# Two combine stages dissolved into the attentions that follow them, a third staging slot, and scores of two head pairs issued together

## The chip, the cores and the metric

One core of one Trainium2 chip runs the whole program in one launch. The time is device microseconds (us) from start to end of an execution; the value compared is the median of several executions of the same kernel. PE is the matmul engine (TensorE), DVE the vector engine, ACT the scalar engine with its function tables, POOL the GpSimd engine, SP the engine that issues most DMAs. SBUF is the on-chip memory, PSUM the eight banks into which PE writes.

## The reference, cut to what matters

Everything is fp32. x is [16 batches, 112 rows, 256], the context is [16, 375, 256]. Eight blocks follow each other, each of the form x = x + block(layernorm(x)):

- L0_xattn, a "focused" linear attention over the context; L0_ffn, a gated mixture of 8 experts, top 2 of them per row, added to the row with softmax weights;
- L1_xattn, an attention whose scores pass a tanh before the softmax ("tanh attention"); L1_ffn, a shared feed-forward with low-rank expert terms;
- L2_xattn, softmax attention with 16 heads of 64 ("wide"); L2_ffn, again 8 experts and top 2, but its sum passes a layernorm of its own;
- L3_xattn, softmax attention with 16 heads of 16 and a mask ("narrow"); L3_ffn, a ternary feed-forward.

The two mixtures, and the norm that follows each:

```python
# L0_ffn: xn = layernorm(x); f = layernorm(xn)*gamma+beta; top 2 experts, weights p
x = x + p0*y[expert0] + p1*y[expert1]   # rows beyond an expert's capacity get 0
# L2_ffn: h = layernorm(x)
x = x + layernorm(h + p0*y[expert0] + p1*y[expert1], eps=1e-12) * ln_w + ln_b
# the next block (L1_xattn or L3_xattn) begins with layernorm(x) of that x
# L3_xattn, per batch and head
scores = q @ k.T / 4
scores = where(mask == 0, -1e9, scores)
out = softmax(scores) @ v
```

## The kernel before, in words

`program` (L2852) runs twelve stages, with a barrier of all engines between two of them (`core.clear`, L115): focused attention, route, run_experts and combine of L0_ffn, tanh attention, shared experts, wide attention, route, run_experts and combine of L2_ffn, narrow attention, ternary feed-forward. Inside a stage each engine has its own program, written out by hand for batch 0 to 15, and semaphores order them. Nothing of the next stage starts before the barrier.

**Routing.** `route` (L2279) normalises x and computes for every row its two experts, its slots in a DRAM buffer and the weights p. `picked` is ready when the experts are chosen; PE then makes the running counts (`cum`, L2540), DVE the slots (`slots_done`), and POOL writes the rows out with 32 indirect DMAs ("puts", L2364). **Experts.** `run_experts` (L2548) reads blocks of rows, runs both matmuls and stores y in DRAM (`ybuf`). **Combine.** `combine` (L2744) fetches each row's two results with 32 indirect DMAs on POOL ("gathers", L2787, two per batch, a ring of four batches), adds them with two scalar_tensor_tensor on DVE (L2812, L2814), and takes the statistics (bn_stats, bn_aggr). For L2_ffn (`norm`) the sum goes to `xf`, one Sqrt on ACT follows when all 16 batches are summed (L2799), and then six DVE instructions a batch (L2827 to L2833) normalise, scale, add ln_b, add x, and take statistics again.

**Keys and values made early.** Later attentions need projections of the context. PE makes them as "parts" in earlier stages, where it has room, ACT copies each part out of PSUM (`take`). `KeysValues` (L2064) keeps those of the narrow attention in SBUF: 4 parts a batch, batches 0 to 9 in route of L2_ffn ("r_"), 10 to 15 in its combine ("c_"). `SpilledKeysValues` (L2142) makes 8 of the 16 batches of the wide attention, 14 parts a batch (8 of K, 6 of V), and stores them in DRAM from two staging slots: batches 0 to 3 in the focused attention, 4 to 6 in route of L0_ffn, 7 in its combine. ACT waits for a slot's earlier store before it writes the slot, and each stage waits for its stores before it ends (`wait_stored`, L2205). In `route` the parts stand in three places of PE's program: one beside each batch (BESIDE), eight before the `cum` matmul (AHEAD), the rest behind it (BEHIND). In route of L2_ffn, DVE also prepares the ternary weights (`tw.prepare`, L1721, two reductions at L1727), and PE sums them (`tw.sum`, L1719) before the last four parts.

**Tanh attention** (L568). ACT takes all deviations in one Sqrt (L661), then per batch six tanh (L679) and six exponentials (L671). PE's program for a batch is scores 0 and 1, transposes of the next batch's x (L751), the projection of batch b-2 (L788), scores, products (L775), the spreading of sums (L783), scores, products. DVE's: normalise the next x (L697), copy its transpose (L703), residual of b-2 (L720 and `keep`, L99), copy the products' sum (L709), reciprocal (L714), divide (L716). POOL builds the masked queries `qbd` (L648) and copies values (L655).

**Narrow attention** (`softmax_attention` with wide False, L830). Per pair of heads PE issues the scores of the pair (L1375, two matmuls of 375 columns on two of four banks), turns the probabilities of earlier heads (L1387, transposes), runs slot jobs (q, x, z, y) and every four heads the products (L1410). `scores` waits until DVE has read the banks of the pair before (`low_done`). DVE takes each head's masked minimum (L1230) and writes the masked scores to `ssb`, a ring of four; ACT takes the exponential (L1165) into `p_sb`, a ring of eight. DVE also copies most turned probabilities (L1241), and once a batch does the residual, divide and normalise. PE's program is:

```python
def body(b, h):
    for pair in range(0, H, 2):
        scores(b, h, pair)
        trail(b, h, pair, LT, turn_p)      # LT = 4 heads behind
        slot_jobs(job, b, h, pair, "kqvxyz")
        trail(b, h, pair + 1, LT, turn_p)
        if (pair - LP) % SIDE == 0:
            trail(b, h, pair, LP, products)  # LP = 8 behind
```

## Time and profile before

| what | value |
|---|---|
| median of three executions | 2900.87 us (2896.5 to 2906.04) |
| profiled execution | 2931.14 us |
| its span in the trace | 2929.4 us |
| mean granted clock of PE | 0.935 of full |
| PE, DVE, ACT, POOL busy | 86%, 47%, 39%, 27% of the span |

Where the stages lie in that span (from the first instructions of each in the trace): focused attention 0 to 310.8 us, route of L0_ffn to 425.8, its experts to 832.5, its combine to 901.8, tanh attention to 1112.5, shared experts to 1274, wide attention to 1905, route of L2_ffn to 2024, its experts to 2296.5, its combine to 2391.8, narrow attention to 2757, ternary feed-forward to the end. The page divides the span in 40 slices of 73 us, and its second part gives the busy tenths of each engine in each slice:

```profile
PE   6999749999956998979999999883999559999786
...
DVE  6988512222232654546643333442111367777665
ACT  4555211111105991234443434331333126666431
POOL 3443140000041210027754444404000401221242
PEclk8999879999977998989999999996999779999898
```

A digit 9 says that the engine was busy for 90% or more of the slice. PE has its weak slices at the routing stages (slices 6 and 28) and at the combines (slices 12, 13, 32 and 33). A busy share says how full an engine is, not what the end of a stage waited for: that is to be read from the chain of instructions in each stage.

### The profile page before, as it was taken

What the parts mean: (1) busy time and instruction counts of PE and PEld (TensorE: products, weight loads), DVE (VectorE), ACT (ScalarE), POOL (GpSimd) and SP (SyncE); (2) the same over time, 40 slices, a digit from 0 to 9 for tenths busy, and PEclk for the clock granted to TensorE, in tenths of its full rate; (3) what the DMA queues carried; (4) which work ended last, traced back from release to release, by engine and by line L of the source; (5) the groups of instructions that cost most, each with busy time, mean ns of one, the idle gap of its engine ahead of it and who ended that gap; (6) DMA issues with size and microseconds to landing.
All of it is one profiled execution on the core that took longest, in us unless ns stands there. A gap on an engine that the chain in (4) does not pass through costs nothing. (4 is left out here: it accounts for less than half of the span.)

```text
span 2929.4 us, 47164 instructions
## 1 busy us (share of the span) xinstructions
PE 2512.4 (86%) x15874; PEld 1754.4 (60%) x15874; DVE 1372.3 (47%) x4867; ACT 1130.7 (39%) x2617; POOL 797.8 (27%) x867
## 2 busy tenths in 40 slices
PE   6999749999956998979999999883999559999786
PEld 4676428888832554647666565562999336666544
DVE  6988512222232654546643333442111367777665
ACT  4555211111105991234443434331333126666431
POOL 3443140000041210027754444404000401221242
PEclk8999879999977998989999999996999779999898
DMA  4222352222023210043310000044888310000000
GB/s 138 82 101 102 133 197 108 93 84 94 24 85 118 67 54 1 1 134 133 113 36 6 11 6 6 1 155 172 322 325 325 127 35 11 8 11 6 1 7 19
DMA packets 69939, 252.57 MB, mean 86 GB/s; under 512 B 16395, under 2 KB 32040, under 8 KB 52264
## 3 DMA queue, kind: packets, MB, share of 16 engines
q1 hardware_dynamic: 60008, 226.24, 22.2%
q0 software_dynamic: 9744, 23.87, 2.6%
q8 instruction: 114, 1.87, 0.3%
q14 instruction: 73, 0.60, 0.1%
HBM read 197.97 MB, written 52.10 MB: 85 GB/s over the span
## 5 line engine op out<-in xcount | busy, mean ns | idle before, releaser
L2732 PE MATMUL L_ffne_up<-L_ffne_xT,L_ffne_wu 128*128 128x128 f32 (+1 forms) x2144 | 389.8, 337 | 7.3 <-DMA L_ffne_wu<-in_L_ffn_up 7.3
L2732 PEld LDWEIGHTS L_ffne_up<-L_ffne_xT,L_ffne_wu 128*128 128x128 f32 x2144 | 328.1, 193 | 54.3 <-DMA L_ffne_wu<-in_L_ffn_up 6.9
L1082 POOL TENSOR_SCALAR L_xattn_p<-L_xattn_p,L_xattn_rec 112x375 f32<-112x375 f32 x256 | 311.8, 1225 | 0.0
L1387 PEld LDWEIGHTS L_xattn_pt<-ident,L_xattn_p 112*125 112x125 f32 x1536 | 197.3, 189 | 166.4 <-ACT L_xattn_p L1165 75.7
L2717 PE MATMUL L_ffne_dn<-L_ffne_wd,L_ffne_hT 128*112 128x256 f32 (+1 forms) x1200 | 266.3, 379 | 1.5 <-issue 1.5
L1387 PE MATMUL L_xattn_pt<-ident,L_xattn_p 112*125 112x112 f32 x1536 | 247.3, 289 | 20.5 <-DVE L_xattn_pt L1241 16.0
L1224 DVE TENSOR_REDUCE L_xattn_least<-L_xattn_s 112x1 f32<-112x375 f32 x256 | 128.4, 543 | 284.7 <-PE L_xattn_s L1375 284.4
L2717 PEld LDWEIGHTS L_ffne_dn<-L_ffne_wd,L_ffne_hT 128*112 128x112 f32 (+1 forms) x1200 | 216.8, 183 | 39.7 <-issue 2.1
L1241 DVE COPY L_xattn_pt<-L_xattn_pt 125x336 f32<-125x336 f32 x448 | 210.6, 497 | 52.6 <-PE L_xattn_pt L1387 52.4
L1165 ACT ACTIVATE L_xattn_p<-L_xattn_s,L_xattn_least 112x375 f32<-112x375 f32 x256 | 145.1, 570 | 186.2 <-DVE L_xattn_least L1224 186.1
L2620 POOL DMA_DIRECT2D L_ffn_ybuf<-L_ffne_y x75 | 40.1, 534 | 641.3 <-DVE L_ffne_y L2670 386.8
L1165 ACT ACTIVATE L_xattn_p<-L_xattn_ssb,L_xattn_least 112x375 f32<-112x375 f32 x256 | 153.8, 602 | 129.9 <-DVE L_xattn_least L1230 129.0
L2642 ACT ACTIVATE L_ffne_sg<-L_ffne_up 128x280 f32<-128x280 f32 x128 | 51.6, 403 | 329.0 <-PE L_ffne_up L2732 329.0
L2644 ACT ACTIVATE L_ffne_hT<-L_ffne_up,L_ffne_b 128x128 f32<-128x128 f32 x280 | 98.9, 366 | 154.9 <-DMA L_ffne_b<-in_L_ffn_b 76.0
L1230 DVE CUSTOM_DVE_ANT_0 L_xattn_ssb<-L_xattn_s,L_xattn_hide 112x375 f32<-112x375 f32 x256 | 130.8, 545 | 57.4 <-issue 37.7
L1080 POOL TENSOR_TENSOR pool_tick<-ident 1x1 f32<-1x1 f32 x128 | 23.4, 183 | 478.7 <-DVE L_xattn_rec L1236 478.7
L1410 PE MATMUL L_xattn_o<-L_xattn_pt,L_xattn_v 125*64 125x112 f32 (+1 forms) x3072 | 153.4, 268 | 0.0
L2688 DVE TENSOR_TENSOR L_ffne_hT<-L_ffne_sg,L_ffne_up 128x280 f32<-128x280 f32 x128 | 57.1, 446 | 189.2 <-ACT L_ffne_sg L2642 189.2
L1410 PEld LDWEIGHTS L_xattn_o<-L_xattn_pt,L_xattn_v 125*64 125x64 f32 (+1 forms) x3072 | 110.1, 118 | 45.8 <-issue 26.2
L1375 PE MATMUL L_xattn_s<-L_xattn_kt,L_xattn_qt 64*112 64x375 f32 x512 | 116.4, 532 | 17.7 <-ACT L_xattn_p L1165 17.7
L671 ACT ACTIVATE ta_pT<-ta_pT,ta_hide_b,ta_cap 125x896 f32<-125x896 f32 x96 | 121.8, 1272 | 0.0
L1375 PE MATMUL L_xattn_s<-L_xattn_kt,L_xattn_qbd 64*112 64x375 f32 x512 | 115.3, 528 | 2.7 <-POOL L_xattn_qbd L1093 2.7
(369 smaller groups left out, 4480.0 us busy)
## 6 DMA issues: line engine op xcount, KB each, us to landing
L_ffne_wd<-in_L_ffn_down SPq DMA_DIRECT2D x43, 1024.0 KB, 4.9
L_ffne_wu<-in_L_ffn_up SPq DMA_DIRECT2D x35, 1024.0 KB, 5.2
L_ffne_wu<-in_L_ffn_up SPq DMA_DIRECT2D x8, 2048.0 KB, 7.9
L_xattn_kt<-L_xattn_kd SPq DMA_DIRECT2D x8, 1500.0 KB, 7.9
L_xattn_v<-L_xattn_vd SPq DMA_DIRECT2D x8, 1500.0 KB
L_ffn_xbuf<-L_ffnr_zeros SPq DMA_DIRECT2D x8, 1120.0 KB, 12.7
fa_ctxT<-in_ctxT SPq DMA_DIRECT2D x16, 375.0 KB, 3.6
fa_rows<-in_ctx_rows SPq DMA_DIRECT2D x16, 375.0 KB
```

The costliest lines, as they stand in the source:

```text
L671: act.activation(p, p, ACT.Exp, bias=hide_b[:, h, c % KT:c % KT + 1], scale=cap[0:KP, :]).then_inc(exp_done, 1)
L1082: p = pool.tensor_scalar(p_sb[:, head % RP, :], p_sb[:, head % RP, :], rec[:, h, head:head + 1], None, ALU.mult)
L1165: act.activation(p_sb[:, head % RP, :], src, ACT.Exp, bias=least[:, h, head:head + 1], scale=-1.0, accum_out=sums[:, h, head:head + 1]).th ...
L1224: dve.tensor_reduce(low, s, AX.X, ALU.min).then_inc(low_done, 1)
L1230: dve.tensor_tensor_reduce(out=ssb[:, head % 4, :], in0=s, in1=hide[:, h, :], scale=1.0, scalar=3e38, op0=ALU.add, op1=ALU.min, accum_out= ...
L1241: dve.tensor_copy(pt_sb[:, head % RP, :, :], pt_ps[head % 2][0:KP, 0, 0:KT * S].rearrange("p (k s) -> p k s", k=KT)).then_inc(pt_done, 1)
L1375: m = pe.matmul(score_ps(b, n)[0:S, 0, 0:SK], q, k, start=True, stop=True)
L1387: m = pe.transpose(pt_ps[head % 2][0:KP, 0, kt * S:(kt + 1) * S], p_sb[:, head % RP, kt * KP:(kt + 1) * KP], ident[0:S, 0:S])
L1410: m = pe.matmul(o_ps[n * VC:n * VC + dh, chunk // 4, chunk % 4 * S:(chunk % 4 + 1) * S], v, pt_sb[:, (head + n) % RP, kt, :], start=(kt == ...
L2644: act.activation(hT[:, h, f, q * RH:(q + 1) * RH], src, ACT.Gelu, bias=b1[:, h, f:f + 1]).then_inc(h_done, 1)
L2717: m = pe.matmul(dn_ps[i][0:TR, 0, 0:D], hT[:, h, f, t * TR:(t + 1) * TR], wd[:, h, f, :], start=(f == 0), stop=(f == FC - 1))
L2732: m = pe.matmul(up_ps[s % RING][k][:, 0, 0:RH], wu[:, h, c, k * FF + f * 128:k * FF + (f + 1) * 128], xT[:, h, c, q * RH:(q + 1) * RH], st ...
```

## The change

**1.** `combine` is gone. `routed_experts` goes on to call tanh_attention or the narrow softmax_attention, and these do its work between their own.
**2.** Tanh attention: POOL gathers the first four batches at its start and then two per batch while b is 0 to 5; DVE adds the experts of four batches first, then two per batch at the end of its body; the Sqrt comes in three groups (batches 0-3, 4-7, 8-15), the second and third between tanh and exponentials of batches 2 and 6.
**3.** Narrow attention: POOL gathers six batches at its start (a ring of three, each gather waits for an addition) and one per batch afterwards. DVE adds the experts of one batch at pair 2 of each batch, and normalises one batch further on at pair 14 or 6 (two scalar_tensor_tensor, bn_stats, bn_aggr); four batches are added and two normalised before the first scores, or around `normalize(0)`. ACT takes two Sqrts every second batch, at head 8. ln_b is no longer added there: route of L2_ffn adds it to x beforehand, with 16 tensor_tensor on DVE after `slots_done` and before `tw.prepare`.
**4.** The masked scores go straight into `p_sb`, now a ring of six, where ACT exponentiates in place; `ssb` is gone, `msk` has one buffer, `onT` shares `o_sb`. DVE's minimum waits for the turn of the head six before, not for an exponential.
**5.** In the narrow attention PE issues the scores of two pairs (four heads, four banks) together at every second pair, and none at the other.
**6.** Parts: the wide attention's batches 4 to 7 (56 parts) all lie in route of L0_ffn, and the narrow attention's batches 0 to 15 (64 parts) in route of L2_ffn; AHEAD is 4 instead of 8. Staging has three slots that live from the focused attention to the end of run_experts, where alone the stores are waited for; V is stored in three DMAs per batch instead of one. `tw.sum` comes after 12 parts of BEHIND.
**7.** Loops over batches in the two attentions (each_batch, with a hardware loop over the middle batches) are written out.

The diff, cut to its core:

```diff
-def tanh_attention(core, sw):
+def tanh_attention(core, r, sw):
+        RING, OPENING = 4, 4
+        GROUP = (0, OPENING, 2 * OPENING, NB)
+        def arriving(b):
+            return range(OPENING + 2 * b, min(OPENING + 2 * b + 2, NB))
...
             def _(pool):
+                for b in range(OPENING):
+                    gather(b)
...
+                    for later in arriving(b):
+                        gather(later)
+                for b in range(NB):
+                    body(b, b % 2)
...
-                act.activation(core.std[:, :], mv[:, :, 1], ACT.Sqrt, bias=core.eps[0:S, :]).then_inc(std_done, 1)
+                def deviations(n):
+                    act.wait_ge(stats_done, n + 1)
+                    span = slice(GROUP[n], GROUP[n + 1])
+                    act.activation(core.std[:, span], mv[:, span, 1], ACT.Sqrt, ...)
+                deviations(0)
...
+                        if c == 2 and b in (2, 6):
+                            deviations(1 if b == 2 else 2)
...
+                def add_experts(b):
+                    h = b % 2
+                    dve.wait_ge(got_in[b % RING], 32 * (b // RING + 1))
+                    ch.link(dve.scalar_tensor_tensor(out=half[:, h, :], in0=got[:, b % RING, 0, :], ...
+                    dve.scalar_tensor_tensor(out=x[:, b, :], in0=got[:, b % RING, 1, :], ...).then_inc(summed, 1)
+                    dve.wait_ge(summed, b + 1)
+                    ch.link(dve.bn_stats(core.st46[:, h, :], x[:, b, :]))
+                    ch.link(dve.bn_aggr(mv[:, b, :], core.st46[:, h, :]))
...
                     if b > 0:
                         take_o(b - 1, 1 - h)
                         divide(b - 1, ch)
+                    for later in arriving(b):
+                        add_experts(later)
+                for b in range(OPENING):
+                    add_experts(b)
                 normalize(0, 0)
...
 def softmax_attention(...):
+    PP = 8 if wide else 6
...
+                        if not wide and head == 8 and b % 2 == 0 and b + 2 < NB:
+                            root(b // 2 + 1)
+                            if b + 4 < NB:
+                                root_of_sums(b // 2 + 2)
...
+                def beside(b, pair):
+                    if pair == 0 and b == 0:
+                        add_experts(4)
+                    if pair == 2 and 5 + b < NB:
+                        add_experts(5 + b)
+                    if b == 0 and pair in (4, 6):
+                        add_normed(pair // 2)
+                    if b % 2 == 0 and pair == 14 and b + 4 < NB:
+                        add_normed(b + 4)
+                    if b % 2 == 1 and pair == 6 and b + 4 < NB:
+                        add_normed(b + 4)
...
-                        after(dve, exp_done, b * H + head - 3)
+                        after(dve, t_out, b * H + head - PP + 1)
-                        dve.tensor_tensor_reduce(out=ssb[:, head % 4, :], in0=s, in1=hide[:, h, :], scale=1.0,
+                        dve.tensor_tensor_reduce(out=at_p(b, head), in0=s, in1=hide[:, h, :], scale=1.0,
...
+                if not wide:
+                    for b in range(2):
+                        add_experts(b)
+                    for b in range(2):
+                        add_normed(b)
                 normalize(0, 0)
                 normalize(1, 1)
+                if not wide:
+                    for b in range(2, 4):
+                        add_experts(b)
...
                 def body(b, h):
                     for pair in range(0, H, 2):
-                        scores(b, h, pair)
+                        if wide:
+                            scores(b, h, pair)
+                        elif pair % 4 == 0:
+                            scores(b, h, pair)
+                            scores(b, h, pair + 2)
...
-        self.spans = {"r_": (0, 10), "c_": (10, NB)}
+        self.spans = {"r_": (0, NB)}
...
 class SpilledKeysValues:
+    SLOTS = 3
     def store_values(self, sp, b):
-        sp.wait_ge(self.done, (b - self.first + 1) * len(self.parts))
-        sp.dma_start(self.vd[b], self.vs[:, b % 2, :, :]).then_inc(self.v_stored[b % 2], 16)
+        for kt in range(KT):
+            sp.wait_ge(self.done, (b - self.first) * len(self.parts) + self.IC + 2 * kt + 2)
+            sp.dma_start(self.vd[b, :, kt, :], self.vs[:, b % self.SLOTS, kt, :]).then_inc(...)
...
 def route(...):
-        BESIDE, AHEAD = parts[0:NB], parts[NB:NB + 8]
-        BEHIND = parts[NB + 8:]
+        BESIDE, AHEAD = parts[0:NB], parts[NB:NB + 4]
+        BEHIND = parts[NB + 4:]
...
+                if not twice:
+                    for b in range(NB):
+                        c.step(dve.tensor_tensor(x[:, b, :], x[:, b, :], after_b[:, :], ALU.add))
                 if tw:
                     tw.prepare(dve, lg_ps[0])
...
-                    if tw and n == len(BEHIND) - 4:
+                    if tw and n == 12:
                         tw.sum(pe, lg_ps[0])
...
 def run_experts(...):
+                if spilled:
+                    spilled.wait_stored(sp)
...
-def combine(core, pre, r, norm, keys):
...
-    spilled = SpilledKeysValues(core, "L2_xattn", {"a_": (0, 4), "r_": (4, 7), "c_": (7, 8)})
+    spilled = SpilledKeysValues(core, "L2_xattn", {"a_": (0, 4), "r_": (4, 8)})
```

## Rows read from the trace of the kernel before

**Rows 1.** Windows by stage: length, busy PE, PEld, DVE, ACT, POOL, then PEclk, DMA share, GB/s.

```profile
832.50:901.80 69.30, 31.11 (x56) 13.63 (x56) 24.86 (x64) 7.45 (x14) 29.84 (x32) 0.67 0.31 103
...
940.00:1070.00 130.00, 126.35 (x1510) 66.43 (x1509) 80.37 (x116) 130.00 (x137) 33.13 (x48) 1.00 0.26 85
2296.50:2391.80 95.30, 40.58 (x120) 25.73 (x120) 59.65 (x162) 14.13 (x26) 30.46 (x32) 0.70 0.24 71
2440.00:2740.00 300.00, 285.01 (x2829) 191.75 (x2826) 226.69 (x973) 182.40 (x576) 57.11 (x53) 0.99 0.03 8
2757.00:2929.40 172.40, 122.69 (x496) 71.75 (x496) 104.75 (x201) 44.13 (x83) 57.75 (x41) 0.89 0.04 11
```

**Rows 2.** Waits in the first combine stage (832 to 902 us).

```profile
PE L_xattnkvc_ps L2228 <- issue: 12.3, 2, 6.8
```

**Rows 3.** Timeline of the first combine stage; start, duration, engine and line.

```profile
838.21 0.48 DVE L2812 SCALAR_TENSOR_TENSOR L_ffnc_half<-L_ffnc_got,L_ffn_p,x_sb 112x256 f32<-112x256 f32 x1 [11.47 <-DMA L_ffnc_got<-L_ffn_ybuf,L_ffn_get]
...
888.32 0.29 SPq L2195 DMA_DIRECT2D L_xattn_vd<-L_xattnkvc_vs  x1
```

**Rows 4.** Timeline of the second combine stage.

```profile
2305.45 0.48 DVE L2812 SCALAR_TENSOR_TENSOR L_ffnc_half<-L_ffnc_got,L_ffn_p,L_ffn_xf 112x256 f32<-112x256 f32 x1 [8.31 <-issue]
...
2307.05 0.45 DVE L2812 SCALAR_TENSOR_TENSOR L_ffnc_half<-L_ffnc_got,L_ffn_p,L_ffn_xf 112x256 f32<-112x256 f32 x1
```

**Rows 5.** Timeline of the first routing stage, PE.

```profile
357.29 7.83 PE L2224 MATMUL L_xattnkvr_ps<-L_xattnkvctxT,L_xattnkvwk 128*128 128x375 f32 x24
...
368.39 0.38 PE L2540 MATMUL L_ffnr_cum<-L_ffnr_picked,L_ffnr_before 112*112 112x128 f32 x2
```

**Rows 6.** Timeline of the first routing stage, ACT, and the next stage's opening.

```profile
404.05 0.60 ACT L2248 ACTIVATE L_xattnkvr_vs<-L_xattnkvr_ps 125x512 f32<-125x512 f32 x1 [7.15 <-remote]
426.27 1.28 ACT L2642 ACT_TABLE_LOAD   x1 [21.63 <-PEq L117]
```

**Rows 7.** Timeline of the second routing stage.

```profile
1961.90 0.38 PE L2540 MATMUL L_ffnr_cum<-L_ffnr_picked,L_ffnr_before 112*112 112x128 f32 x2
...
1973.78 4.47 DVE L1727 TENSOR_REDUCE tw_wsum<-tw_w 128x1 f32<-128x2048 f32 x2
...
1984.01 0.38 ACT L2137 ACTIVATE L_xattn_v<-L_xattnkvr_ps 125x256 f32<-125x256 f32 x1 [0.27 <-PE L_xattnkvr_ps L2122]
```

**Rows 8.** Timeline of the opening of the tanh attention.

```profile
903.61 0.31 ACT L661 ACTIVATE std<-mv,eps 112x16 f32<-112x16 f32 x1
...
903.94 1.28 ACT L663 ACT_TABLE_LOAD   x1
...
904.24 0.41 DVE L697 TENSOR_SCALAR ta_xn<-x_sb,mv,rstd 112x256 f32<-112x256 f32 x1
...
913.50 3.35 PE L760 MATMUL ta_s_ps<-ta_qbd,ta_kT 64*125 64x448 f32 x8 [8.16 <-DMA ta_ctxr<-in_ctx_rows]
```

**Rows 9.** Timeline inside the tanh attention.

```profile
938.08 0.41 PE L751 MATMUL ta_xt_ps<-ident,ta_xn 112*128 112x112 f32 x2
...
947.92 0.41 DVE L697 TENSOR_SCALAR ta_xn<-x_sb,mv,rstd 112x256 f32<-112x256 f32 x1
```

**Rows 10.** Timeline of PE late in the tanh attention.

```profile
1080.46 1.02 PE L760 MATMUL ta_s_ps<-ta_qbd,ta_kT 64*125 64x448 f32 x4
1081.41 1.02 PE L783 MATMUL ta_fin_ps<-ta_o_sb,ta_spread 128*128 128x448 f32 x2
1082.36 1.77 PE L760 MATMUL ta_s_ps<-ta_qbd,ta_kT 64*125 64x448 f32 x8
1084.06 1.17 PE L775 MATMUL ta_o_ps<-ta_pT,ta_vaug 125*32 125x112 f32 x40
```

**Rows 11.** Timeline of the opening of the narrow attention, DVE.

```profile
2402.38 0.74 DVE L1214 TENSOR_SCALAR L_xattn_xn<-x_sb,mv,rstd 112x256 f32<-112x256 f32 x2
2409.83 0.54 DVE L1230 CUSTOM_DVE_ANT_0 L_xattn_ssb<-L_xattn_s,L_xattn_hide 112x375 f32<-112x375 f32 x1 [6.72 <-POOL L_xattn_hide L1097]
```

**Rows 12.** Line L1093 (POOL, two per batch), 2430 to 2720 us.

```profile
L1093 POOL TENSOR_TENSOR L_xattn_qbd<-L_xattn_qt,halfmask x28: 932/932/934, 2432.8 to 2712.0; 128x448 f32<-128x448 f32 x28
```

315 lines of the change are left out of this document (160 added, 155 removed).

## The prediction

> **What bounds the kernel now.** I read first the windows by stage [rows 1]. The second column is PE's busy time: 285 of 300 us in the middle of the narrow attention, but 31.1 of 69.3 us in the first combine and 40.6 of 95.3 in the second. No other engine is full there either (DVE 24.9 and 59.7, POOL 29.8 and 30.5), so a combine is bound by a chain, and 164.6 us of the span pass in stages that no engine fills. In the middle of the tanh attention ACT is busy 130.00 of 130 us and DVE 80.4: ACT is the bound, DVE has room. In the narrow attention PE bounds, DVE follows with 226.7 of 300.
>
> Then the timelines of the combines. The first has its last store issued at 888.32 [rows 3], and then nothing for some 13 us until the barrier at 901.8: a store's landing is waited for. PE loses 12.3 us there to "issue", waits that nothing in the profile explains [rows 2]. The first addition comes 5.7 us after the stage's start (838.21) [rows 3], in the second combine 9 us after it (2305.45), and one batch's addition with statistics takes 1.60 us there (2305.45 to 2307.05) [rows 4].
>
> **Against which time the sum is made.** The profiled execution took 2931.1 us (span 2929.4, 1.7 around it), 30 us or 1.0% more than the median of 2900.9. Savings are read from the profile and taken from the median; what that does to them comes at the end.
>
> **The first combine goes: -69.3 us** [rows 1]. What it did comes back in three places.
> *Its 14 parts of K and V* go to the route stage. There six K parts take 7.83 us, 1.3 each, and `cum` waits for the eight AHEAD parts until 368.39 [rows 5]. With four, all K, they end near 357.3 + 5.2 = 362.5, so `cum`, slots and the 32 puts come about 5.5 us earlier. PE's parts: ACT ended its last copy 21.6 us before 426.27, at 404.65, and had waited 7.15 us for a staging slot [rows 6]. The third slot takes that wait away: 397.5, and 14 parts more (8 x 1.3 and, by 512 columns for 375, 6 x 1.8: 21 us) make about 418.5. The puts set the end now, and with them it comes 5.5 us earlier, at 421; the parts fit below. The stores of the last batch then land beside the first weights of the experts, which may wait up to 3 us, and each V store is three issues instead of one, which SP has time for. Net -2 us (between -6 and +3).
> *The opening of the tanh attention.* Now the Sqrt comes at once (903.61) and the first scores at 913.50, after loads [rows 8]. After the change the first addition is at S + 5.7, the gathers give a batch each 2.5 us (two of 29.84 / 32 = 0.93 us [rows 1] and what lies between issues), so four batches are summed at about S + 5.7 + 7.5 + 1.6 = S + 14.8. Behind that come Sqrt and reciprocal (0.6), normalise and transposes (904.24 to 905.34, where PE's 8.16 us of waiting begin: 1.1), the copy and the masked queries (0.4 and 2 x 0.93 [rows 12]), with hand-overs 4.8; scores at S + 19.6 instead of S + 11.7. +8 us. What stands behind the gathers on POOL later, the next batch's masked queries, needs DVE's copy anyway, which comes after the additions the gather waits for: 0.
> *The steady part.* A batch takes ACT 130 x 12 / 137 = 11.4 us [rows 1]. DVE and PE form a loop beside it: transposes at 938.08, then residual, divide, and the next normalise at 947.92, which ends at 948.33: 10.3 us [rows 9]. For batches 1 to 5 (DVE's body of batch 0 has little else) two additions of 1.6 us with little waiting enter this loop: 13.5 to 13.7, more than ACT's 11.4, or about +2 us in each of five batches, 9.3 with what batch 0 keeps. The two added Sqrt blocks (a table load, 0.31 us, a load back: 1.28 + 0.31 + 1.28 = 2.9 by [rows 8]) cost 5.8 us of the full engine, a part of it where ACT waits for DVE anyway: 3.7. Together +13, between 0 (the scores of a batch run two batches deep and hide the loop) and +20.
>
> **The second combine goes: -95.3 us** [rows 1].
> *Its 24 parts, and the added ln_b* in route. `cum` comes at 1961.90 now, 5 us earlier with four parts fewer; DVE starts its two reductions at 1973.78 (4.47 us both), and ACT's last copy is at 1984.01 [rows 7], 40 us before the stage ends at 2024: the puts set its end. They will end 5 us earlier. But 24 parts of 1.3 us are 31 us, and the 16 added tensor_tensor (as long as the 0.45 us instruction of [rows 4], 7 us) stand before the reductions, so that `tw.sum` after 12 parts waits from about 1973.5 to 1980. PE ends near 1984.4 + 31 + 6.5 = 2022, a copy and the barrier later. Net 0 (-3 to +3).
> *The opening of the narrow attention.* First minimum now at 2409.83, normalise at 2402.38 [rows 11], which is S + 18.0 and S + 10.6. After: the first sums at S + 9, two batches summed and normalised need 4 x 1.6 us of DVE, a Sqrt of sums and a Sqrt of deviations between them with waits there and back (together some 10 us), so normalise at about S + 20, 9.5 later. On POOL the masked queries of batch 0 stand behind the sixth gather, which waits for the third addition, after both normalises: another 1. +10.5 us (6 to 15).
> *The steady part.* Masked queries are built at 2432.8 and, as the last of 28, at 2712.0 [rows 12]: less the second of the pair's own microsecond, 278.2 / 13 = 21.4 us a batch, of which PE is busy 20.3 [rows 1]. Joined scores: in the tanh attention, where both forms occur, four matmuls take 0.95 us to the next instruction (1080.46 to 1081.41) and eight take 1.70 (1082.36 to 1084.06) [rows 10], so a join saves 0.20 us. Four joins a batch: -0.8, PE 19.5. DVE is busy 16.2 a batch (226.7 / 14) and gains 1.6 + 1.6 + 0.1 in batches 0 to 11: 19.5 too. Two engines that are equally full and wait for each other every pair do not both run at 19.5: now PE at 20.3 with DVE at 16.2 loses 1.1. I take 22.2 for batches 1 to 11 (+0.8 each, 9), +3 for batch 0, -0.5 for each of the last four: +10. The low end is a perfect cover, -0.8 in 12 batches, about -10; the high end one and a half 1.6 us blocks laid bare in each batch, +26. ACT's seven pairs of Sqrt (3.2 us each with loads) are hidden: it is busy 182.4 of 300; without that cover they cost 22. In-place exponentials, ring of six, one `msk`: 0, since minima wait for the turn six heads back, long past; if not, they are part of the high end. Written-out loops: 0.
>
> **Sum.** -2 - 69.3 + 8 + 13 + 0 - 95.3 + 10.5 + 10 = **-125**. From 2900.9 that gives 2776. The stalls without cause in the combines [rows 2] may belong to the profiled execution alone; if all of its extra 30 us lay there, only 95 would be saved, 2806. I add 4: **2780**.
>
> **Rule and row on table loads.** Row: the Sqrt ends at 903.92 and the next load starts at 903.94 and takes 1.28 us [rows 8]; a switch costs 1.3 us and nothing in front of it. The Trainium skill (ScalarE: Activation LUTs, What ACT_TABLE_LOAD costs) gives 1283 ns for the load and some 1380 ns for a drain, 2.66 us a switch. The load's length agrees with the trace, the drain shows in no row here, and since ACT had just emptied itself the row does not exclude it. The rule speaks against the change, which adds 18 switches; by it the saving would be 18 to 25 us smaller.
>
> **Rivals.**
> *A, DVE late in both attentions* (0.20). For: both covers are thin by the sums above, and DVE's waits for the gathers stand in front of its minima and copies. Then tanh gives back 20 and narrow 26, with the opening at 15: +28, about 2808.
> *B, full cover* (0.15). For: an added block of 1.6 us is shorter than PE's time for a pair of heads (21.4 / 8 = 2.7), and scores run up to four heads ahead. Then tanh +3 and narrow -8: 2752.
> *C, slower* (0.02): PE's granted clock falls in the narrow attention, because PE now waits for DVE in every pair. Price: PE's work there (some 320 us: 20.3 in each of 16 batches) at 1.2 instead of 2.4 GHz are 320 us more, 3100. It decides from 121 + 9 = 130 us on, that is if over 40% of that work runs at half clock. Against it: a stage in which PE is busy only 71% (122.7 of 172.4) still has a clock of 0.89 [rows 1].
> *D, switches cost double* (0.05): an in-front drain of the same length as the load. Four in the tanh attention, where ACT is full, +5, and some 10 of the 14 in the narrow one laid bare with their neighbours' waits: +13, so about 2798. This is what the rule above would do.
> *E, the join does nothing* (0.03): the second pair's banks are not read yet when PE comes to it, so PE waits for `low_done` where it used to turn. Then 0.8 in each of 16 batches is not saved (13) and some 7 of waiting come on top: 2800.
> The forecast has 0.55. A measurement of this kernel tells 0.3% (9 us) from no change: faster 0.97, same 0.01, slower 0.02.
>
> **Range.** From B's 2750 to 2815: A, D and E lie in it, and so do the bounds of the openings; out are C, a deeper B, and A together with profile-only stalls (2834).
>
> **What would show it.** Right: no stage between experts and tanh scores; first tanh scores about 20 us after the stage's start; ACT waiting for PE's scores in batches 1 to 5 with a period near 13.5, 11.4 after; route of L2_ffn still 119 us with PE waiting before L1719's line; narrow period 22 while DVE adds, under 21 in the last four; eight 375-column matmuls in one run of 1.7 us. Wrong: an experts stage that starts late, a granted clock under 0.9 in the narrow attention, or periods there above 23.

## The result, and where the time went

The kernel after takes 2862.09 us (median of four, 2856.36 to 2867.74), beside 2902.11 for the kernel before (four, 2896.5 to 2906.04): ratio 0.9863 [0.9836, 0.9891]. It is faster, by 40 us and not by 121: the interval leaves out 1, though the gain is less than 2%. 2862 lies above the range.

**One thing has to be known before traces are compared.** Every set of runs below ran on one chip, and the sets fall into two groups: the kernel before takes 2902 to 2904 us in one (call it place A) and 2931 to 2935 in the other (place B). Whether B is another chip or a condition of one is not known: e1 to e4 (B) and e5 to e8 (A) bear the same chip number, 4, the other sets of B bear 15, 13 and 6, and whether such a number names one piece of hardware from set to set is not said. The profiled execution shown ahead of the prediction is of B (2931.1), that of the kernel after is of A (2856.36). So the kernel before was profiled again in A (e6) and the change in B (e18). Lengths of the stages, in us, each from the first instructions after its barrier:

| stage | before, A (e6) | after, A (e5) | before, B (rows of before) | after, B (e18) |
|---|---|---|---|---|
| route of L0_ffn | 113.5 | 116.6 | 114.9 | 136.2 |
| its experts | 407.8 | 428.9 | 406.6 | 415.2 |
| its combine | 49.5 | none | 69.4 | none |
| tanh attention | 211.4 | 236.7 | 211.2 | 238.1 |
| wide attention | 634.2 | 631.5 | 630.8 | 632.7 |
| route and experts of L2_ffn | 389.9 | 393.5 | 391.7 | 405.8 |
| its combine | 84.9 | none | 95.2 | none |
| narrow attention | 364.0 | 406.6 | 365.5 | 404.1 |
| span | 2902.5 | 2860.0 | 2929.4 | 2881.9 |

In A the first four rows add up to 782.2 before and 782.2 after: dissolving the first combine brought nothing. A gain as large as the whole 42.5 us lies in the last two rows above the span, 448.9 before and 406.6 after; what the rows beside them add and take away (3.6 more in the second route with its experts, 2.7 less in the wide attention, and small differences in the stages not shown) cancels.

Each length is from one profiled execution. How much it moves by itself is seen where a run's edit leaves a stage alone: in B the experts took 415.0 to 415.9 us, the tanh attention 237.4 to 238.3 and the narrow one 402.1 to 404.4; in A 426.7 to 431.9, 235.6 to 240.2 and 401.6 to 406.7.

The windows of the kernel after, by stage (columns as in [rows 1]), with the tanh attention, the narrow attention and two stretches inside it, with and without additions:

```profile
853.30:1089.32 236.02, 186.70 (x2112) 97.25 (x2112) 134.95 (x227) 194.43 (x204) 77.50 (x99) 0.92 0.28 83
2277.14:2682.92 405.78, 341.33 (x3240) 238.89 (x3240) 317.73 (x1251) 231.53 (x689) 102.34 (x96) 0.90 0.07 20
2330.00:2530.00 200.00, 175.11 (x1740) 123.38 (x1729) 171.82 (x674) 122.53 (x371) 55.81 (x53) 0.95 0.07 19
2570.00:2670.00 100.00, 93.69 (x962) 66.87 (x958) 79.58 (x336) 64.75 (x198) 18.47 (x17) 0.98 0.03 7
```

The reader is to see PE at 175.11 of 200 where it was at 285 of 300 [rows 1]: the narrow attention is no longer bound by PE while DVE adds. And the granted clock, the third number from the end, is 0.95 there, where it was 0.99.

The same view of the kernel before in A (e6): the two combines and the narrow attention.

```profile
837.00:886.46 49.46, 23.68 (x56) 12.01 (x56) 24.45 (x64) 7.46 (x14) 30.12 (x32) 0.71 0.44 145
2282.75:2367.61 84.86, 36.93 (x120) 25.13 (x120) 59.99 (x162) 14.15 (x26) 30.43 (x32) 0.70 0.27 80
2367.61:2731.57 363.96, 331.69 (x3240) 221.88 (x3240) 259.38 (x1107) 209.96 (x660) 69.07 (x65) 0.97 0.04 11
```

The combines are 134.3 us together and not 164.6 [rows 1]; the busy times of DVE, ACT and POOL are nearly the same, and PE's are longer in B at a lower clock (31.1 and 40.6 us at 0.67 and 0.70, against 23.7 and 36.9 at 0.71 and 0.70). Most of what B has more is idle time. In the first combine it looks like this (the trace of before, PE):

```profile
855.72 3.78 PE L2228 MATMUL L_xattnkvc_ps<-L_xattnkvwv,L_xattnkvctxT 128*125 128x512 f32 x4 [5.56 <-issue]
866.26 3.78 PE L2228 MATMUL L_xattnkvc_ps<-L_xattnkvwv,L_xattnkvctxT 128*125 128x512 f32 x4 [6.76 <-issue]
877.56 7.95 PE L2228 MATMUL L_xattnkvc_ps<-L_xattnkvwv,L_xattnkvctxT 128*125 128x512 f32 x11 [7.53 <-ACT L_xattnkvc_vs L2248]
```

**The experts' late opening.** SP's queue in the kernel after, from the last stores of keys and values to the first loads of the experts (start, duration of the issue), and then PE's first work in the experts:

```profile
408.49 1.24 SPq L2342 DMA_DIRECT2D L_xattn_kd<-L_xattnkvks  x1
412.04 13.15 SPq L2347 DMA_DIRECT2D L_xattn_vd<-L_xattnkvvs  x3
426.95 4.33 SPq L2755 DMA_DIRECT2D L_ffne_rows<-L_ffn_xbuf  x1
433.38 6.70 SPq L2760 DMA_DIRECT2D L_ffne_wd<-in_L_ffn_down  x1
```

The same V stores one by one (shortest, median and longest issue in ns), then PE:

```profile
L2347 SPq DMA_DIRECT2D L_xattn_vd<-L_xattnkvvs x5: 250/250/6282, 395.1 to 418.9; - x5
```

```profile
417.65 0.59 PE L2379 MATMUL L_xattnkvr_ps<-L_xattnkvwv,L_xattnkvctxT 128*125 128x512 f32 x1
450.00 2.88 PE L2862 MATMUL L_ffne_t<-ident,L_ffne_rows 112*128 112x112 f32 x10 [31.75 <-DMA L_ffne_rows<-L_ffn_xbuf]
```

The first two V stores take 0.25 us each and wait for their parts in between; the last, issued at 418.9, takes 6.28 us and ends at 425.2, 7 us after PE's last part, so the barrier stands where it stood. Behind it the first issue of rows takes 4.33 us and the third issue 6.70. The experts' rows land only for a first transpose at 450.00, 23 us after the stage's start. In the trace of before that gap was 4.4, from 426.3 on:

```profile
430.72 2.87 PE L2705 MATMUL L_ffne_t<-ident,L_ffne_rows 112*128 112x112 f32 x10 [34.45 <-DMA L_ffne_rows<-L_ffn_xbuf]
```

The last store of the kernel before was issued in the combine, beside a stage that waited anyway.

**The tanh attention.** Its opening, DVE's first addition, and PE's first scores, then PE's transposes of two batches in the steady part:

```profile
863.19 0.48 DVE L723 SCALAR_TENSOR_TENSOR ta_half<-ta_got,L_ffn_p,x_sb 112x256 f32<-112x256 f32 x1 [16.25 <-DMA ta_got<-L_ffn_ybuf,L_ffn_get]
```

```profile
875.59 1.86 PE L808 MATMUL ta_s_ps<-ta_qbd,ta_kT 64*125 64x448 f32 x4 [2.58 <-POOL ta_qbd L664]
...
930.14 0.41 PE L799 MATMUL ta_xt_ps<-ident,ta_xn 112*128 112x112 f32 x2 [2.46 <-DVE ta_xn L743]
943.90 0.41 PE L799 MATMUL ta_xt_ps<-ident,ta_xn 112*128 112x112 f32 x2 [2.46 <-DVE ta_xn L743]
```

The first scores come 22.3 us after the stage's start of 853.3 (19.6 was forecast, 11.7 it was). In the steady part a batch takes 13.8 us, and PE waits 2.5 us in it for DVE's normalise; 13.5 to 13.7 was forecast. ACT around the first of the two added Sqrts:

```profile
905.78 1.12 ACT L695 ACTIVATE ta_pT<-ta_pT,ta_hide_b,ta_cap 125x896 f32<-125x896 f32 x1
906.92 1.28 ACT L683 ACT_TABLE_LOAD   x1
908.21 0.30 ACT L683 ACTIVATE std<-mv,eps 112x4 f32<-112x4 f32 x1
908.53 1.28 ACT L703 ACT_TABLE_LOAD   x1
```

**The narrow attention: two batches, two clocks.** Windows of the kernel after, each from one batch's masked queries to the next's (L1159), and under them a short stretch of the second:

```profile
2435.16:2457.70 22.54, 20.06 (x214) 14.32 (x207) 20.07 (x80) 12.88 (x42) 6.53 (x7) 1.00 0.06 16
2457.70:2482.72 25.02, 21.92 (x201) 15.30 (x199) 19.80 (x80) 15.92 (x46) 6.35 (x7) 0.86 0.07 20
2476.00:2478.50 2.50, 2.50 (x9) 1.39 (x10) 2.43 (x7) 1.41 (x5) 1.46 (x2) 0.50 0.00 0
```

DVE has 20 us of work in both (16.1 in the kernel before). The long batch has a granted clock of 0.86: from about 2475 to 2482 PE runs at 1.2 GHz. What PE did before the clock fell is in the timelines of DVE and PE there:

```profile
2470.04 0.43 DVE L1405 TENSOR_TENSOR xs<-xs,x_sb 112x256 f32<-112x256 f32 x1
...
2471.65 0.48 DVE L1323 SCALAR_TENSOR_TENSOR L_ffn_xf<-L_ffn_xf,mv,L_xattn_ln_w 112x256 f32<-112x256 f32 x1
2472.17 0.48 DVE L1325 SCALAR_TENSOR_TENSOR x_sb<-L_ffn_xf,L_xattn_rstd,x_sb 112x256 f32<-112x256 f32 x1
...
2474.36 0.92 DVE L1378 COPY L_xattn_pt<-L_xattn_pt 125x336 f32<-125x336 f32 x2
```

```profile
2468.70 1.52 PE L1517 MATMUL L_xattn_s<-L_xattn_kt,L_xattn_qbd 64*112 64x375 f32 x8
...
2475.01 1.57 PE L1529 MATMUL L_xattn_pt<-ident,L_xattn_p 112*125 112x112 f32 x6 [3.06 <-DVE L_xattn_pt L1378]
2476.51 2.85 PE L1517 MATMUL L_xattn_s<-L_xattn_kt,L_xattn_qbd 64*112 64x375 f32 x8
```

The waits of PE for these copies, 2330 to 2530 us (us in total, times, longest):

```profile
PE L_xattn_pt L1529 <- DVE L_xattn_pt L1378: 24.6, 18, 3.2
```

In even batches `add_normed` stands at pair 14 behind normalise and the residual of the batch before. The copies of probabilities wait behind all three, PE stands 3.06 us, its clock falls to half, and the same eight score matmuls take 2.85 us instead of 1.52. In odd batches the pieces stand apart, PE never waits that long, and the clock stays at 1.00.

Is it the wait that the fall follows? The longest waits of PE from batch 2 to batch 14, beside the falls of the clock, each 3.4 or 6.8 us long:

| run | longest waits of PE | how many of them a fall follows |
|---|---|---|
| after; e18 (the same kernel) | five of 3.1 to 3.2 us in each | all ten |
| e8 | five of 2.4 to 2.5 us | all five |
| e14 | five of 1.9 to 2.0 us | three |
| e17, e6, e13 | none over 1.4 us | none |

So the fall belongs to these waits, but the length of a wait alone does not decide it: of e14's five nearly equal waits two have no fall behind them, nor has one of 2.2 us in batch 1 of e17, and the trace of before has one fall of 3.4 us behind a wait of 1.36 us.

The additions are also longer than the instruction they were priced by. One of DVE's groups in the kernel after, 2330 to 2530 us (busy time, then mean ns of one):

```profile
L1307 DVE SCALAR_TENSOR_TENSOR L_ffn_xf<-L_xattn_got,L_ffn_p 112x256 f32<-112x256 f32 x9 | 10.3, 1144 | 0.3
```

The instruction of L1307 takes 0.49 us each time in the opening and 1.14 us each time in the steady part, where it begins beside POOL's 1.12 us tensor_tensor of `widen` (L1173), which becomes free at the same point of the batch:

```profile
2405.97 1.12 POOL L1173 TENSOR_TENSOR L_xattn_rec_w<-L_xattn_rec,one 112x512 f32<-112x512 f32 x1 [14.70 <-DVE L_xattn_rec L1373]
```

```profile
2406.24 1.14 DVE L1307 SCALAR_TENSOR_TENSOR L_ffn_xf<-L_xattn_got,L_ffn_p 112x256 f32<-112x256 f32 x1
```

The Trainium skill (SBUF — State Buffer, SBUF: two separate sides) says that a VectorE operation with two SBUF inputs and a GpSimd operation that reads SBUF share one pair of ports, which whoever starts first holds for its whole instruction. The rows agree in kind: alone DVE's instruction would have ended at 2406.72; it ends at 2407.38, 0.29 us behind POOL's, which ends at 2407.09. They do not show that all of its work waited, since 0.48 us from 2407.09 on would end at 2407.57. The two instructions of a normed addition (L1323, L1325) are longer, too, in each second batch, where they begin beside POOL's masked queries: 0.8 and 0.6 us.

### The profile page after: what moved, and what is told of

Same layout as the page of the kernel before. It is cut to its first block and busy times, and to the rows that moved or that the text cites. A ratio compares the mean times of both kernels' runs of the same rounds, so it can differ in the third digit from the quotient of the medians.

```text
span 2854.6 us, 46446 instructions
## 1 busy us (share of the span) xinstructions
PE 2507.7 (88%) x15874; PEld 1765.5 (62%) x15874; DVE 1375.6 (48%) x4867; ACT 1158.1 (41%) x2651; POOL 801.9 (28%) x867
## 5 line engine op out<-in xcount | busy, mean ns | idle before, releaser
L1529 PE MATMUL L_xattn_pt<-ident,L_xattn_p 112*125 112x112 f32 x1536 | 254.0, 295 | 39.9 <-DVE L_xattn_pt L1378 36.2
L1249 ACT ACTIVATE L_xattn_p<-L_xattn_p,L_xattn_least 112x375 f32<-112x375 f32 x256 | 153.7, 601 | 126.3 <-DVE L_xattn_least L1367 126.0
L1139 POOL TENSOR_TENSOR pool_tick<-ident 1x1 f32<-1x1 f32 x128 | 23.4, 183 | 480.7 <-DVE L_xattn_rec L1373 480.7
L1367 DVE CUSTOM_DVE_ANT_0 L_xattn_p<-L_xattn_s,L_xattn_hide 112x375 f32<-112x375 f32 x256 | 131.0, 545 | 16.8 <-issue 12.1
L695 ACT ACTIVATE ta_pT<-ta_pT,ta_hide_b,ta_cap 125x896 f32<-125x896 f32 x96 | 113.8, 1189 | 0.0
```

Of the source, the lines that this page charges most:

```text
L695: act.activation(p, p, ACT.Exp, bias=hide_b[:, h, c % KT:c % KT + 1], scale=cap[0:KP, :]).then_inc(exp_done, 1)
L1249: act.activation(at_p(b, head), src, ACT.Exp, bias=least[:, h, head:head + 1], scale=-1.0, accum_out=sums[:, h, head:head + 1]).then_inc(e ...
L1367: dve.tensor_tensor_reduce(out=at_p(b, head), in0=s, in1=hide[:, h, :], scale=1.0, scalar=3e38, op0=ALU.add, op1=ALU.min, accum_out=low).t ...
L1529: m = pe.transpose(pt_ps[head % 2][0:KP, 0, kt * S:(kt + 1) * S], at_p(b, head)[:, kt * KP:(kt + 1) * KP], ident[0:S, 0:S])
```

## The experiments

Ratios are against the kernel before in the same set of runs. e1 to e4, e9 to e12, e13 to e16 and e17, e18 ran in place B, e5 to e8 in A.

**e1, the kernel before once more.** No edit.

> The kernel before, unchanged, in another profiled execution. Theory P (the 30 us by which the profiled execution of before, 2931, exceeded its median, 2902, lay in the unexplained stalls of the two combine stages): span near 2900, second combine stage near 75 us instead of 95, first near 60 instead of 69, all other stages within 1 us. Rival (the profiler makes every stage a little slower): span near 2930 again and both combines as long as in the first trace.

2934.95 us in the one execution, span 2933.2, combines of 67 and 95 us again. So the 164.6 us were no accident of one profiled execution. That the place decides was seen only with e6.

**e2 and e11, the last store of K and V issued from the experts.**

```diff
-            self.store_values(sp, b)
+            if b < self.count - 1:
+                self.store_values(sp, b)
...
+                    if spilled and isinstance(b, int) and b == 1:
+                        spilled.store_last(sp)
```

> The kernel after, but the eighth batch's K and V of the wide attention are stored in the experts stage, behind the loads of its first two experts, instead of at the end of the routing stage. Theory S (the experts of L0_ffn start 19.4 us late because their first rows stand behind 3 MB of stores on SP's DMA queue): the first expert rows reach PE 4 to 5 us after the stage's start instead of 23, the routing stage ends some 5 us earlier, too, since SP is not held while issuing; about -22 us, 2840. Rival (the rows are late because the memory is busy with the puts): below -5 us.

2872.61, ratio 0.9801 [0.9777, 0.9826]. PE in the experts' opening, the stage starting at 450.42:

```profile
455.57 2.87 PE L2872 MATMUL L_ffne_t<-ident,L_ffne_rows 112*128 112x112 f32 x10 [6.55 <-DMA L_ffne_rows<-L_ffn_xbuf]
```

The first transpose comes 5.2 us after the start. Without the edit, in the same place (e18, the stage starting at 452.13), it comes after 10.6:

```profile
462.70 2.88 PE L2862 MATMUL L_ffne_t<-ident,L_ffne_rows 112*128 112x112 f32 x10 [12.46 <-DMA L_ffne_rows<-L_ffn_xbuf]
```

The 23 us above are of place A. The experts take 408 us where e4 beside it takes 415.5. The route stage does not get shorter (135.8): in place B it ends with PE's parts. Repeated in another set:

> The kernel of e2 again, to be read beside e12 and on this chip. e2 gave 0.9801 of before where before took 2933. Where before takes 2902, the routing stage has no stalls and the experts of L0_ffn started 19 us late, so theory S gives -20 to -25 us against the kernel after: 2837 to 2842, ratio 0.977. Rival (the lateness is not the stores): ratio 0.983 to 0.985.

2875.06, 0.9793 [0.9761, 0.9826], experts 407.7. In B the backlog of the store is shown as the cause of the late opening, and by the stage it costs 7 to 8 us; the ratios of whole runs (e18 has 0.9811 [0.9788, 0.9835]) do not tell so little apart. In A, where the route ends 20 us earlier and less time is left for the store to land, the experts are 21 us longer than before the change. That the store is all of it there is argued from the same rows; the edit was not run in A, where e2's and e11's expectations had put 20 us and more.

**e3, V stored in one DMA when all its parts are there.**

```diff
-        for kt in range(KT):
-            sp.wait_ge(self.done, (b - self.first) * len(self.parts) + self.IC + 2 * kt + 2)
-            sp.dma_start(self.vd[b, :, kt, :], self.vs[:, b % self.SLOTS, kt, :])
+        sp.wait_ge(self.done, (b - self.first + 1) * len(self.parts))
+        sp.dma_start(self.vd[b], self.vs[:, b % self.SLOTS, :, :])
```

> The kernel after, but V is stored in one DMA per batch instead of three. Theory S says that volume counts, so the experts still start late: within 6 us of the kernel after. Rival (three DMAs with 4 KB pieces are what fills the queue): the experts start up to 19 us earlier, 2843 to 2855.

2885.01, 0.9849 [0.9829, 0.9868]; experts 419.4 against 415.5 of e4. The number of issues is not what delays the loads: with one issue in place of three, and all of V stored later, they are later still. That leaves the bytes.

**e4, the scores of two pairs apart again.**

```diff
-                        if wide:
-                            scores(b, h, pair)
-                        elif pair % 4 == 0:
-                            scores(b, h, pair)
-                            scores(b, h, pair + 2)
+                        scores(b, h, pair)
```

> The kernel after, but in the narrow attention each pair's scores are issued by themselves, as before. Joining was priced at 0.8 us a batch, and in the last batches of the trace of after a batch takes 20.3 us against 21.4 before, 1.1 less. If PE's time counts in every batch: +13 to +18 us, 2875 to 2880. If DVE bounds in the batches that add experts: +5 or less, all of it in the last four batches.

2895.43, 0.9874 [0.9847, 0.9901], narrow 412.3 against 404.1 in e18: the join gives 8 us, 0.5 a batch. The ratios of the whole runs are further apart (0.9811 for e18, 18 us, give or take 11), so it may be worth somewhat more. Where nothing is added to DVE its batches take 21.5, 21.3 and 20.7 against 21.0, 20.5 and 20.2.

**e5 and e6, the change and the kernel before in one place.** No edits.

> The kernel after, unchanged. The kernel before takes 2902 us beside the first measurement of the change and 2933 beside the runs e1 to e4, so the traces of before and after may come from different chips. Theory P2: on a chip where before takes 2933, PE and ACT wait for each other's semaphores in the stretch of the puts (e4: 391 to 427 us, e2 the same), and the routing stage of L0_ffn takes 133 us instead of 115, that of L2_ffn over 130 instead of 121; total about 2888. On a chip where before takes 2902 neither happens: 2862, within 6 us.

> The kernel before, unchanged, for a trace from the same chip as e5. Theory P2: if it takes 2933, its combine stages are 69 and 95 us long again; if it takes 2902, they are some 30 us shorter together and no other stage differs by more than 3 us. Rival: the difference between chips is spread over all stages.

2859.84, 0.9846 [0.9818, 0.9874], and 2904.18. These made the table above possible. PE in the first combine, e6:

```profile
840.71 13.38 PE L2224 MATMUL L_xattnkvc_ps<-L_xattnkvctxT,L_xattnkvwk 128*128 128x375 f32 x32 [10.79 <-DMA L_xattnkvctxT<-in_ctxT]
853.93 10.46 PE L2228 MATMUL L_xattnkvc_ps<-L_xattnkvwv,L_xattnkvctxT 128*125 128x512 f32 x24
```

In e6 the fourteen parts go through without a gap; in the trace of before PE stops three times among the same parts, for 12.3 us "<- issue" [rows 2] and 7.5 for ACT.

**e7, the normalise of the tanh attention a batch earlier.**

```diff
-                        normalize(b + 1, 1 - h)
                         take_xt(b + 1, 1 - h)
...
+                    if b < NB - 2:
+                        normalize(b + 2, h)
                     for later in arriving(b):
```

> The kernel after, but in the tanh attention DVE normalises batch b+2 ahead of the two additions in its body, instead of batch b+1 at the start of the next body, so that PE's transposes no longer wait for the additions. Theory T (the loop of DVE and PE, 10.3 us, grows by the additions to 13.8 and passes ACT's 11.4): the period in batches 1 to 5 returns to about 11.5, -10 to -12 us against the kernel after. Rival (ACT is bound and the additions only delay it through the masked queries or the gathers on POOL): within 3 us of the kernel after.

2851.32, 0.9823 [0.9797, 0.985], tanh 228.4 against 236.7 (e5), more than that stage moves by itself, though the intervals of the two ratios overlap. The DVE-PE loop of the steady part is real and costs 8 us; transposes now come 11.5 us after each other in most batches, ACT's own pace.

**e8, half of the probability copies of the narrow attention on ACT** (a quarter before).

```diff
-            return not wide and head % 4 == 3
+            return not wide and head % 2 == 1
```

> The kernel after, but in the narrow attention ACT copies every second turned head instead of every fourth: DVE loses four copies of 0.50 us a batch, ACT gains four of 0.43. Theory D (DVE bounds the batches that add experts, 23.3 us against 20.3 without): -1.5 to -2 us in each of eleven batches, -16 to -22 us in all against the kernel after. Rival (the waits for the two Sqrts and their table loads on ACT bound them): 0, or up to +10 as ACT gets fuller.

2854.59, 0.9835 [0.9815, 0.9856], narrow 397.3 against 406.6 (the whole runs differ by 5, within their intervals). Half of what was expected: odd batches fell from 22.5 to 21.7, even ones stayed at 24 to 25 with a clock of 0.86 or 0.93, since the stacked block at pair 14 was still there.

**e9, the added Sqrts of the narrow attention without their table** (an Identity stands in for each Sqrt but the first ones, so deviations are wrong there); **e10, its gathers left out after the opening** (later additions take old rows).

```diff
-                    act.activation(std3[:, span], core.mv2[:, span, 1], ACT.Sqrt, bias=tiny[:, :])
+                    act.activation(std3[:, span], core.mv2[:, span, 1], ACT.Sqrt if n < 2 else ACT.Identity, bias=tiny[:, :])
```

```diff
-                    if OPENING + b < NB:
-                        gather(OPENING + b)
```

> The kernel after, but in the narrow attention the Sqrts beside the batches (twelve of two columns each, from the second pair of deviations on) are Identity instead, which needs no other table; what is left out is the square root of those variances. In e8 four copies less on DVE shortened only every second batch (22.5 to 21.7) and left the others at 24 to 25. Theory W (in every second batch ACT's two table loads with the Sqrts between them stand before the exponentials that PE waits for, 3.2 us with 1 to 2 of them laid bare): the long batches fall from 24.6 to about 22.5, -12 to -15 us. Rival (DVE's second block, add_normed behind the residual, makes them long): under -4.

> The kernel after, but in the narrow attention POOL gathers only the first six batches; the others are added from what those left in the ring, so their expert results are left out. The second scalar_tensor_tensor of the additions took 1.14 us on average beside POOL's work in the trace of after, 0.48 elsewhere. Theory G (the gathers hold DVE up, some 0.7 us a batch): -5 to -8 us. Rival (the lengthening comes from POOL's tensor instructions, or is hidden): within 3 us.

2880.55, 0.9821 [0.9789, 0.9853], and 2882.45, 0.9828 [0.9799, 0.9857]. Batches stay at 22.5 and 23.3 to 25.0 in both, the stage at 403.6 and 405.0. Neither the table loads nor the gathers cost anything there that these lengths could show.

**e12, the first half of the kernel as before** (first combine, tanh attention, two staging slots), the second as changed.

```diff
-        spilled = SpilledKeysValues(core, "L2_xattn", {"a_": (0, 4), "r_": (4, 8)})
+        spilled = SpilledKeysValues(core, "L2_xattn", {"a_": (0, 4), "r_": (4, 7), "c_": (7, 8)})
...
+                combine(core, pre, r, False, keys)
```

> Only the second half of the change: L2_ffn's combine dissolved into the narrow attention, joined scores, all its K and V in the routing stage; all of L0_ffn, its combine and the tanh attention as in the kernel before. By the traces of e5 and e6 the first half changes the stretch up to the shared experts by +3 - 3 - 1 = -1 us and the second half brings all of the -42. Theory N (the first half is worth nothing as it stands): 2860 to 2864 where before takes 2902. Rival (it is worth the 20 to 40 us that the sums by stage in the prediction gave it): 2880 to 2900.

2889.55, 0.9854 [0.9821, 0.9887]; e18 has 0.9811 [0.9788, 0.9835]. In B the first half is worth some 13 us by stages (802 before, 789 in e18) and 13 by the ratios, whose intervals overlap; in A it is worth nothing by stages.

**e13, DVE's added work beside the scores left out** (sums of batches 4 to 15, normed additions of 2 to 15; gathers, Sqrts and waits stay).

```diff
+                def skip_experts(b):
+                    dve.wait_ge(got_in[b % RING], 32 * (b // RING + 1))
+                    dve.sem_inc(summed, 1)
...
-                        add_experts(5 + b)
+                        skip_experts(5 + b)
```

> Leaves out the added work of DVE beside the scores of the narrow attention (the sums of batches 4 to 15 and the normed additions of batches 2 to 15 and their statistics); gathers, Sqrts and all waits stay. Theory (DVE's added instructions lie on the path): every batch takes 20.0 to 20.8 us, as the last four of the change do, and the narrow attention falls from about 404 to 370 to 376 us. Rival (the waits, gathers and Sqrts are what costs, the work itself is covered): periods stay over 22 and the stage over 395 us.

2841.32, 0.9683 [0.9668, 0.9698], narrow 362.6 against 404.1. Batches of 20.2 and 20.7, and PE is the bound again:

```profile
2400.00:2500.00 100.00, 94.30 (x999) 67.05 (x995) 80.46 (x345) 69.12 (x209) 29.45 (x28) 1.00 0.08 20
```

So the 41 us come with DVE's added instructions and what follows from them, the fallen clock included; with the gathers, Sqrts and waits in place the batches take what the last ones of e18 take without them.

**e14, the same work at other pairs.**

```diff
-                    if b % 2 == 0 and pair == 14 and b + 4 < NB:
-                        add_normed(b + 4)
-                    if b % 2 == 1 and pair == 6 and b + 4 < NB:
-                        add_normed(b + 4)
+                    if b % 2 == 1 and pair == 4 and b + 3 < NB:
+                        add_normed(b + 3)
+                    if b % 2 == 1 and pair == 10 and b + 4 < NB:
+                        add_normed(b + 4)
```

> All work is kept; the normed addition of even batches moves from pair 14 of the even turn to pair 4 of the odd one, and that of odd batches from pair 6 to pair 10. Theory S (stacking): the long batches fall from 24.5 to about 23, and a pair of batches from 47 to 45.5 us: narrow 8 to 10 us shorter. Theory T (the sum of DVE's work on the path): a pair of batches stays at 47 us within 0.5, the long one only moves, and the stage stays within 3 us.

2878.68, 0.9809 [0.9794, 0.9824], no difference from e18 by the ratio; narrow 396.3, 8 us shorter and below all that this stage took in B with the additions left where they were: by its lengths nearer to S. Batches of 21.5 alternate with 23.5 (clock 1.00) and 25.0 to 26.4 (0.93, 0.87). Of the five long ones three still have a fallen clock, where all five had. What is left of the waits is at pair 4, and it is the port again: the normed addition there begins beside POOL's masked queries (L1159, 2411.01 to 2412.84), and its two instructions take 1.25 and 1.04 us.

```profile
2410.98 1.25 DVE L1323 SCALAR_TENSOR_TENSOR L_ffn_xf<-L_ffn_xf,mv,L_xattn_ln_w 112x256 f32<-112x256 f32 x1
2412.26 1.04 DVE L1325 SCALAR_TENSOR_TENSOR x_sb<-L_ffn_xf,L_xattn_rstd,x_sb 112x256 f32<-112x256 f32 x1
```

```profile
2415.10 0.89 PE L1517 MATMUL L_xattn_s<-L_xattn_kt,L_xattn_qbd 64*112 64x375 f32 x4 [1.91 <-DVE L_xattn_least L1367]
```

Over batches 3 to 12 e14 takes 229.6 us and e18 233.4; with (1 - clock) x length taken off, the most that the half clock can cost, 222.7 and 221.5: the work is worth about the same, as theory T has it (one of e14's blocks falls just behind this stretch, for 1 us), and what differs is the clock. The end of the stage shows it by itself. The last window of e18 and of e14, the same instructions in both:

```profile
2663.80:2710.20 46.40, 39.97 (x386) 28.94 (x378) 29.96 (x124) 21.43 (x65) 5.36 (x5) 0.89 0.01 1
```

```profile
2658.20:2700.70 42.50, 35.96 (x386) 25.84 (x378) 29.94 (x124) 21.37 (x65) 5.36 (x5) 0.99 0.00 1
```

3.9 us for a clock of 0.89 against 0.99. The waits of PE before the fall in e18 are the same in e14 (0.9, 0.5 and 1.0 us), so why the clock falls here in one and not in the other is not known, and half of e14's 8 us may be luck.

**e15, the first two additions ahead of the bias** of the narrow attention.

```diff
+                    for b in range(2):
+                        add_experts(b)
                     dve.wait_ge(w_in, NLOADS * 16)
...
                     dve.wait_ge(bias_done, 1)
-                    for b in range(2):
-                        add_experts(b)
                     for b in range(2):
                         add_normed(b)
```

> In the narrow attention's opening DVE adds batches 0 and 1 ahead of the wait for the bias instead of behind it. Theory (the bias wait delays the first sums): the first addition comes at about S + 9 instead of S + 12.4, the first minimum at S + 27 instead of S + 30, and the run is 3 us shorter. Rival (the first gather lands as late as that by itself, or Wo and mask loads share its queue): first addition at S + 12 or later, nothing gained.

2882.51, 0.9813 [0.9794, 0.9833], no difference from e18 by the ratio; the stage shows it: first addition at S + 8.0, first minimum at S + 25.7 instead of S + 29.7, stage 399.9 instead of 404.1.

**e16, e2, e7, e8, e14 and e15 together, and `tw.sum` after 20 parts instead of 12; e17, the same without the late `tw.sum`; e18, the change as given.**

```diff
-                    if tw and n == 12:
+                    if tw and n == 20:
                         tw.sum(pe, lg_ps[0])
```

> The change with six edits: last store of K and V issued from the experts, normalise of tanh a batch earlier, half of the pt copies of the narrow attention on ACT, tw.sum 8 parts later, additions spread, bias behind the first two additions. By the parts measured alone: store -9 to -20, normalise -8, copies -9, tw.sum -3, spread and bias -3 to -12, together 32 to 50 us below the change as given: 2810 to 2830 us on the chip where before takes 2903, or ratio 0.968 to 0.975. Rival (the copies on ACT and the spread additions save the same waits): ratio 0.977 to 0.981.

> e16 with tw.sum back behind 12 parts. Theory (the late tw.sum moved DVE's and PE's work into the puts, where hand-overs stall on this chip): route and experts of L2_ffn take 408 us again instead of 416, the run 2836, ratio 0.966. Rival (chance in one profiled execution): 416 stays, the ratio is that of e16, 0.9685.

> The change as given, beside e17 on the same chip. By e4, e9 and e10 its ratio on the chip where before takes 2933 should be 0.983 to 0.985 (2885 us); experts of L0_ffn 415, tanh 237, narrow 404. If it is 0.98 or less, the edits of e17 brought less than their stages say.

e16: 2843.05, 0.9685 [0.9672, 0.9698]. e17: 2838.56, 0.9681 [0.9659, 0.9704]. e18: 2878.31, 0.9811 [0.9788, 0.9835]. The mended change is 40 us faster than the change on the same chip, 92 faster than the kernel before. Narrow in e17: 373.2 us, its third to twelfth batch between 20.5 and 22.0 us. Its window from 2334 to 2622:

```profile
2334.00:2622.00 288.00, 265.43 (x2756) 188.26 (x2756) 240.84 (x985) 210.29 (x642) 76.82 (x72) 1.00 0.06 17
```

The clock never falls there, with all the additions in place: once ACT has half of the copies and no block of DVE is longer than PE's store of work, the rest of the added work costs about 0.9 us a batch (42.6 a pair against 40.9 in e13). Which of e17's edits does it was not tried one by one beyond e8 and e14, neither of which is enough alone. The late `tw.sum` is not resolved (e16 and e17 overlap; the stages were 416 and 410, e18 406).

## Why the prediction was wrong

The sign of the whole was right, and of every term but one: the route with the experts got longer and not shorter. In one place (A, e6 to e5) the gain is 42.5 us, so the forecast of 121 promised 78.5 too much. The five items below make 82; the other stages, forecast at 0, came out 4 shorter.

- **The combines' length, 26 us.** The sum took 164.6 us out [rows 1]. In the place where the result was taken they are 134.3. The prediction saw "stalls without cause" [rows 2], gave all 30 us of them a case (2806), and then chose "I add 4". That choice failed: the row said that PE lost 12.3 us to nothing the profile shows, the profiled execution lay 30 us above the median, and the two belong together. The 7.15 us wait of [rows 6], read as a wait for a staging slot, was such a stall, too; in e6 the same copies wait 1.12. That PE's parts then ended in A where the forecast had them (below) is luck: the third slot took no wait away there, since there was none.
- **The route stage and the experts, 26 us.** Forecast -2, measured +24 (route +3.1, experts +21.1). The puts did come about 5 us earlier (last one issued at 413.5 against 418.7) and PE's parts ended at 418.2 (forecast 418.5). The failed step is that the experts' first weights "may wait up to 3 us" for the last stores and that SP "has time for" three issues: the last V issue alone takes 6.28 us, so the barrier does not move, and then the experts' rows stand behind 3 MB of K and V and are there 23 us after the start instead of 4.4. "An experts stage that starts late" stood among the signs of being wrong, and it is what came.
- **The tanh attention, 4 us.** +25.3 for +21. Scores at S + 22.3 for S + 19.6, because the first gather lands at S + 9.9 and not S + 5.7; period 13.8 for 13.5 to 13.7. The loop of [rows 9] was the right reading, and e7 takes 8 us of it back.
- **The second route, 4 us.** +3.6 for 0: PE stands 4.97 us before `tw.sum`, as said, but with the 24 parts behind it PE, and no longer the puts, sets the end of the stage: its last part ends at 2002.5 and the last put at 1991.8, with the experts starting at 2004.8.
- **The narrow attention, 22 us.** +42.6 for +20.5. Opening +11.2 (forecast +10.5; the bias adds 4 to it, e15). The join: -0.8 was forecast; e4, which takes back the join alone, gives 0.5 to 0.8 a batch where DVE has nothing added (from before to after it is 0.9 to 1.0, with the in-place exponentials in it: 42.6 a pair in e6, 40.7 to 40.9 in e5 and e13). About right. Batches 3 to 12: 23.4 a batch instead of 22.2. Take off at most 1.4 a batch for the clock (granted 0.86 or 0.93 in each second batch) and 22.1 is left, what the forecast had. DVE's additions cost 3.9 a batch and not 3.3, L1307's 0.66 us beside POOL more. The first two batches got 11.2 us longer and not 4, at clocks of 0.53 and 0.87 (0.62 and 1.00 in e6), and the last batch got 1 longer instead of 0.5 shorter, with up to 5 us of half clock in it. The failed step is the one against rival C: it looked at the clock of a whole stage (71% busy, still 0.89) and priced C only as an entire attention at half clock. A partial loss had no price: five falls of 3.4 to 6.8 us behind single waits of 3.1 us. Together the parts put down to the half clock are up to 24 us, as much as the whole miss of this stage; that is a bound, worked out from (1 - clock) x length. Rival A (DVE late) was nearest in kind, and for the narrow attention in size as well: 26 and 15 for the opening, 42.6 measured. Its +28 over both attentions is a third of the 78.5. Of the signs of being wrong, periods above 23 came in each second batch; the stage's clock, named at under 0.9, was 0.90.
- The rivals B, D and E are out: B by the periods, D by e9 for the narrow attention (no batch shortened when the switches went) and by ACT's rows for the tanh attention, E by the eight-matmul runs of 1.52 us.

Against the rule weighed in the prediction (the Trainium skill, ScalarE: Activation LUTs, What ACT_TABLE_LOAD costs), the runs speak for the row: e9 shows no price at all for the switches in the narrow attention, where ACT waits anyway, and in the tanh attention, where ACT is full, the exponential ends at 906.90 and the load starts at 906.92, so that the Sqrt with both loads takes 2.9 us. The load's length agrees with the 1283 ns that the Trainium skill gives there; its drain does not show, and the measurement decides.

**What stays open.** Why PE and ACT stall in place B while POOL issues its series of indirect DMAs in routes and combines, and in no trace of A. The stalls move with the work: once the parts stand beside the puts, the route stage has them. PE in e18, POOL's puts running from 380.0 to 419.9:

```profile
400.49 3.78 PE L2379 MATMUL L_xattnkvr_ps<-L_xattnkvwv,L_xattnkvctxT 128*125 128x512 f32 x4 [3.15 <-issue]
408.13 3.78 PE L2379 MATMUL L_xattnkvr_ps<-L_xattnkvwv,L_xattnkvctxT 128*125 128x512 f32 x4 [3.87 <-issue]
418.63 3.78 PE L2379 MATMUL L_xattnkvr_ps<-L_xattnkvwv,L_xattnkvctxT 128*125 128x512 f32 x4 [6.72 <-issue]
```

That is why in B the route stages are 20 and 12 us longer after the change than in A, and why the 30 us of stall that leave with the combines are not gained there: 32 come back in the routes. That the indirect DMAs are the cause is argued from where the stalls lie, and was not tried.

## What to carry to other kernels

A stage taken out at its measured length is only as good as that length: where a stage idles for reasons that the profile does not show, and the profiled execution is longer than the median by about as much, take the stage at what its chain explains. Work moved off a stage and onto a vector engine beside a full TensorE is paid twice, once in its own time and once in the clock, if it is put in one block: ask of each block whether it is longer than the work that TensorE has in store, and place the pieces where they stand alone, away from POOL's tensor instructions too. And a transfer that used to end beside an idle stage has a price when that stage goes: its bytes stand in front of the next stage's first loads.

## What the runs showed of the hardware

The granted clock fell to half at a wait of PE of 3.06 us between full stretches, and PE worked at 1.2 GHz for 6.8 us before it rose (3.4 us at others); four such waits and falls in 200 us made 0.95 of the clock. Waits of 2.4 us had the same behind them (e8, five of five), waits of 1.9 us in three of five (e14). This had looked harmless because a stage's mean hides it. The Trainium skill (TensorE: Matmul & The Clock Gate, HAM oscillation — how this bites in real kernels) describes such falling and rising between waits for DMAs; here it is a wait for DVE that does it, and the trace agrees in kind.

A DVE instruction with two SBUF inputs took 1.14 us instead of 0.48 when it began beside a POOL tensor_tensor, and 1.25 beside two (e14); once it took 3.28 us in the tanh attention (L725 at 880.93), across a gather, two tensor_tensor and copies of values. The gathers themselves did not matter: without them (e10) each of the instructions beside `widen` still takes 1.14 us, and beside a gather alone they take 0.48 to 0.49 (L1305, L1307 in the opening).

A table load followed the instruction before it within 0.02 us and took 1.28 us, on an engine that was full. The last batch's stores of K and V (3 MB) ahead of the next stage's loads cost 7 to 8 us of that stage in place B (e2, e11).
